# Decoder layer with a mixture of experts on one core: expert loads tied to the landing of a scatter-add, and a gate-up product on unsplit 32-bit operands

## The reference

```python
logits = x @ gate_weight.T                       # 4096 tokens, 128 router columns, 48 kept experts
top_v, top_i = jax.lax.top_k(probs, TOP_K)       # 8 experts of each token, weights normalised
valid = pos < CAP                                # at most 192 tokens of each expert are kept
xb = xb.at[flat_e, pos_c].set(x[tok])[:, :CAP]   # (48, 192, 512)
gu = jnp.einsum('ech,eoh->eco', xb, gate_up_proj)    # (48, 192, 384)
g, u = jnp.split(gu, 2, axis=-1)
h = jax.nn.silu(g) * u
out = jnp.einsum('eci,ehi->ech', h, down_proj)       # (48, 192, 512)
final = jnp.zeros_like(x).at[tok].add(y * w[:, None])
```

## Time and profile before

| | us |
|---|---|
| median of 3 runs (1283.92 to 1286.0) | 1284.0 |
| the profiled execution, its own time | 1285.87 |
| span of the profile | 1284.1 |
| first scatter-add issued | 869.58 |
| VectorE busy, ScalarE busy, TensorE busy over the span | 881.9, 605.8, 1057.7 |

### The profile page before, as it was taken

One profiled execution on the slowest core, in us unless ns is written; L12 is line 12 of the kernel. 1 busy time (PEld: TensorE's weight loads), 2 busy tenths in 40 slices (PEclk: granted clock), 3 DMA queues, 4 the chain that ended last, 5 costly groups with the idle time before them and its releaser, 6 DMA issues.

```text
span 1284.1 us, 24553 instructions
## 1 busy us (share of the span) xinstructions
PE 1057.7 (82%) x6474; PEld 851.7 (66%) x6474; DVE 881.9 (69%) x2462; ACT 605.8 (47%) x1703; POOL 538.5 (42%) x529
## 2 busy tenths in 40 slices
PE   6985898988888988898899897349888888889892
PEld 5773766766766766776677675248777777777682
DVE  5893776777777776777677775437767777777682
ACT  4542344344444443434444444136655666566561
POOL 2123554455455454454445555622332333333233
PEclk9997998899999998889899997669989999999997
DMA  8986335233222112111211211038989999999983
GB/s 304 341 287 243 141 140 179 105 143 139 83 65 80 44 41 75 48 41 41 82 41 41 74 33 39 12 117 252 259 232 256 229 238 253 242 266 247 257 214 49
DMA packets 80110, 191.80 MB, mean 149 GB/s; under 512 B 23175, under 2 KB 23175, under 8 KB 79568
## 3 DMA queue, kind: packets, MB, share of 16 engines
q1 hardware_dynamic: 44112, 130.70, 31.5%
q0 software_dynamic: 31344, 40.07, 14.8%
q10 hardware_dynamic: 4624, 20.68, 4.8%
HBM read 122.30 MB, written 121.87 MB: 190 GB/s over the span
## 4 chain that ended last, share of the span: by engine, by line
issue 37%; POOL 23%; DMA 23%; DVE 8%; PE 3%; POOLq 2%; ACT 1%; another core or an unknown queue 1%; DVEq 0%; SPq 0%; ACTq 0%
DMA layer_out<-qk_both,scatter_idx 20%; POOL slot_records L493 12%; POOL rstd L504 5%; POOL layer_out L539 3%; DVE qk_both L901 3%; DVE diff L896 2%; POOL qk_rot L517 2%; POOL rstd_h L521 1%; DMA slot_records<-row,slot_idx 1%; PE ps L1222 1%; DMA w_raw<-slot_records 1%; PE ps L1083 1%; PE ps L1068 0%; DMA w_raw<-in_weights 0%
## 5 line engine op out<-in xcount | busy, mean ns | idle before, releaser
L493 POOL DMA_INDIRECT slot_records<-row,slot_idx x256 | 257.2, 1005 | 93.1 <-issue 83.8
L539 POOL DMA_INDIRECT layer_out<-qk_both,scatter_idx x96 | 138.1, 1438 | 293.2 <-DVE scatter_idx L1002 224.9
L504 POOL TENSOR_TENSOR rstd<-mv,neg_half 128x1 f32<-128x1 f32 x96 | 79.6, 829 | 256.9 <-DVE mv L842 99.5
L553 ACT ACTIVATE xn_t<-ps 128x512 f32<-128x512 f32 x64 | 38.3, 599 | 177.1 <-PE ps L1068 146.6
L1083 PE MATMUL ps<-w_high,xn_high 128*128 128x512 f32 x384 | 113.4, 417 | 0.7 <-ACT xn_high L553 0.7
L1222 PE MATMUL ps<-w_high 128*128 128x192 f32 x576 | 92.9, 284 | 24.3 <-DVE w_low L988 23.7
L1083 PE MATMUL ps<-w_high,heads_high 128*128 128x512 f32 x128 | 50.1, 527 | 75.3 <-ACT heads_high L553 71.2
L1083 PE MATMUL ps<-w_high,xn_low 128*128 128x512 f32 x384 | 110.1, 409 | 0.0
L1083 PE MATMUL ps<-w_low,xn_high 128*128 128x512 f32 x384 | 108.3, 404 | 0.0
L1222 PEld LDWEIGHTS ps<-w_high 128*128 128x128 f32 x576 | 79.1, 197 | 40.9 <-issue 39.7
L592 ACT ACTIVATE probs<-ps,neg_max_s 128x128 f32<-128x128 f32 x256 | 90.0, 377 | 13.5 <-DVE neg_max_s L798 11.9
(11 more groups left out here) (164 smaller groups left out, 2613.7 us busy)
## 6 DMA issues: line engine op xcount, KB each, us to landing
gu_sb<-in_gate_up SPq DMA_DIRECT2D x48, 768.0 KB
dn_both<-in_down_proj SPq DMA_DIRECT2D x48, 512.0 KB
slot_records<-dn_both ACTq DMA_DIRECT2D x1, 20196.0 KB, 95.9
w_raw<-slot_records SPq DMA_DIRECT2D x48, 420.8 KB
x_ln<-in_x SPq DMA_DIRECT2D x32, 256.0 KB
x_res<-in_x SPq DMA_DIRECT2D x32, 256.0 KB
ctx_t_sb<-in_ctx_t SPq DMA_DIRECT2D x32, 256.0 KB
ctx_sb<-in_ctx_rows SPq DMA_DIRECT2D x32, 256.0 KB
```

Of the source, the lines that this page charges most:

```text
L493: pool.indirect_dma_start(out=records, out_offset=bass.IndirectOffsetOnAxis(ap=slot_idx[:, s.parity, k:k + 1], axis=0), in_=row[:, s.parit ...
L504: pool.tensor_tensor(rstd[:, :], mv[:, 1:2], neg_half[:, 0:1], ALU.pow).then_inc(steps.sem, 1)
L539: pool.indirect_dma_start(out=out, out_offset=bass.IndirectOffsetOnAxis(ap=scatter_idx[:, d.parity, h:h + 1], axis=0), in_=y[:, d.parity, ...
L553: act.activation(dst, src, ACT.Copy).then_inc(steps.sem, 1)
```

## The change

1. Gate-up on unsplit operands. `gu_high`, `gu_low`, `rows_high` and `rows_low` are gone. ScalarE copies the first half of the transposed rows from PSUM to `rows_t` and VectorE the second half; TensorE multiplies `gu_sb` by `rows_t` in 12 matmuls of plain 32-bit numbers.
2. Loads. SP waits until the scatter-add of e - 4 has landed, and then issues in one train the gate-up weights of e, the down weights of e and the rows of e + 1. `gu_sb` is free when the gate-up product of e - 2 is done.
3. GpSimd's waits ahead of the scatter-add stand in another order, the wait for the last scatter-add behind the others.

```diff
             def load_gate_up(e):
                 if e.back(2).exists():
-                    sp.wait_ge(wgu_v.sem, wgu_v.after(e.back(2), "low"))
+                    sp.wait_ge(gup_t.sem, gup_t.after(e.back(2), "second"))
...
-            load_gate_up(Batch(1, 0, E))
-            with sp.Fori(1, E // 2 - 1) as pair:
-                for off in range(2):
-                    load_gate_up(Batch(pair, off + 1, E))
-                    load_rows(Batch(pair, off, E))
-                    load_down(Batch(pair, off, E))
+            load_rows(Batch(1, 0, E))
+            def load_for(e):
+                if e.back(4).exists():
+                    sp.wait_ge(d_add[e.parity], moved(e.back(4), 2))
+                    settled(sp)
+                load_gate_up(e)
+                load_down(e)
+                if e.next().exists():
+                    load_rows(e.next())
+            for off in range(2):
+                load_for(Batch(1, off, E))
+            with sp.Fori(2, E // 2 - 1) as pair:
                 for off in range(2):
-                load_rows(Batch(E // 2 - 1, off, E))
-                load_down(Batch(E // 2 - 1, off, E))
+                    load_for(Batch(pair, off, E))
+                load_for(Batch(E // 2 - 1, off, E))
...
                     if d.back(1).exists():
                         pool.wait_ge(d_add[d.back(1).parity], moved(d.back(1), 2))
-                    pool.wait_ge(dwn_a.sem, dwn_a.after(d, "y0"))
-                    pool.wait_ge(dwn_v.sem, dwn_v.after(d, "y1"))
-                    pool.wait_ge(dwn_i.sem, dwn_i.after(d, "index"))
...
                 if t.exists():
-                    act.wait_ge(d_gu[t.parity], moved(t, 1))
-                    copy(gu_high[:, t.parity, :, :], gu_sb[:, t.parity, :, :], wgu_a)
...
-                    left_by(gu_low[:, t.parity, :, :], gu_sb[:, t.parity, :, :],
-                            gu_high[:, t.parity, :, :]).then_inc(wgu_v.sem, 1)
...
-                        pairs = [(gu_high, rows_high), (gu_high, rows_low), (gu_low, rows_high)]
+                        return product(dst, lambda k: gu_sb[:, u.parity, k, cols], lambda k: rows_t[:, u.parity, k, :])
```

More of the change, by code:

```diff
@@ L59, in back, with next @@
         return Batch(self.pair, self.off - n, self.limit)
+    def next(self):
+        return Batch(self.pair, self.off + 1, self.limit)
 class Steps:
@@ L212, in decoder_layer @@
         weight_of = [sb("weight_even", [HS, 2]), sb("weight_odd", [HS, 2])]
+        rows_t = w_raw[:, :, :, :].rearrange("p a c n -> p (a c n)")[:, 4 * ROW:4 * ROW + 2 * KC * CAP]\
+            .rearrange("p (e c n) -> p e c n", e=2, c=KC)
         def split_buffers(w):
@@ L216, in split_buffers @@
             at = 0
-            for parts, *shape in ((P, 2, KC, 2 * INTER), (P, 2, KC, CAP), (P, 2, 1, DM), (P, 2, 1, DM),
-                                  (P, 2, 1, CAP), (P, 2, 1, CAP)):
+            for parts, *shape in ((P, 2, 1, DM), (P, 2, 1, DM), (P, 2, 1, CAP), (P, 2, 1, CAP)):
                 size = int(np.prod(shape))
@@ L359, in decoder_layer @@
         s_paced = {nc.vector.engine: sem("vector_paced"), nc.gpsimd.engine: sem("pool_paced"),
-                   nc.scalar.engine: sem("scalar_paced")}
+                   nc.scalar.engine: sem("scalar_paced"), nc.sync.engine: sem("sync_paced")}
         def settled(eng):
@@ L530, in expert_turn @@
                 if d.exists():
+                    pool.wait_ge(dwn_i.sem, dwn_i.after(d, "index"))
+                    pool.wait_ge(dwn_a.sem, dwn_a.after(d, "y0"))
+                    pool.wait_ge(dwn_v.sem, dwn_v.after(d, "y1"))
                     if d.back(1).exists():
                         pool.wait_ge(d_add[d.back(1).parity], moved(d.back(1), 2))
-                    pool.wait_ge(dwn_a.sem, dwn_a.after(d, "y0"))
-                    pool.wait_ge(dwn_v.sem, dwn_v.after(d, "y1"))
-                    pool.wait_ge(dwn_i.sem, dwn_i.after(d, "index"))
                     settled(pool)
@@ L670, in expert_turn @@
                 if t.exists():
[L671 to L676, removed]
+                    act.wait_ge(ffn_t.sem, ffn_t.after(t, "rowsT0"))
+                    if t.back(2).exists():
+                        act.wait_ge(gup_t.sem, gup_t.after(t.back(2), "second"))
+                    copy(rows_t[:, t.parity, :, 0:HS], ps[:, 0, 0:KC * HS].rearrange("p (c n) -> p c n", c=KC), ffn_a)
                 if u.exists():
@@ L1013, in expert_turn @@
                 if t.exists():
[L1014 to L1021, removed]
+                    dve.wait_ge(ffn_t.sem, ffn_t.after(t, "rowsT1"))
+                    if t.back(2).exists():
+                        dve.wait_ge(gup_t.sem, gup_t.after(t.back(2), "second"))
+                    dve.tensor_copy(rows_t[:, t.parity, :, HS:CAP],
+                                    ps[:, 1, 0:KC * HS].rearrange("p (c n) -> p c n", c=KC)).then_inc(ffn_v.sem, 1)
                 if u.exists():
@@ L1211, in expert_turn @@
                 if u.exists():
-                    pe.wait_ge(wgu_v.sem, wgu_v.after(u, "low"))
-                    pe.wait_ge(ffn_v.sem, ffn_v.after(u, "low1"))
+                    pe.wait_ge(d_gu[u.parity], moved(u, 1))
+                    pe.wait_ge(ffn_a.sem, ffn_a.after(u, "copied0"))
+                    pe.wait_ge(ffn_v.sem, ffn_v.after(u, "copied1"))
                     if u.back(1).exists():
@@ L1232, in expert_turn @@
                         if t.back(1).exists():
-                            pe.wait_ge(ffn_v.sem, ffn_v.after(t.back(1), f"low{h}"))
+                            if h == 0:
+                                pe.wait_ge(ffn_a.sem, ffn_a.after(t.back(1), "copied0"))
+                            else:
+                                pe.wait_ge(ffn_v.sem, ffn_v.after(t.back(1), "copied1"))
                         for c in range(KC):
```

18 lines of the change are left out of this document (4 added, 14 removed).

## The result

The changed kernel takes 1333.6 us in the median of 4 runs (1332.3 to 1335.7), the kernel before 1284.35 us in 4 runs. The ratio is 1.0383, interval 1.0363 to 1.0402. It is slower, as predicted; the prediction said 1347. The profiled execution's span is 1330.5 us against 1284.1, 46.4 us more.

What follows compares the result with a forecast made beforehand. Bound: a serial DMA chain of 48 scatter-adds, each delayed by loads ahead. Periods of 10.0 us against 8.56, over 44 periods, add 63 us to 1285.9, giving 1349, or 1347 in the median; range 1265 to 1390.

Steps and rivals of the forecast that it cites:

- The first way of adding it up: Expert-stage period: to first data 1.1, loads 5.5, scatter-add 2.6, last packet to landing about 0.6, together 9.8 us.
- the sum: Expert-stage period added from first-data delay, loads, scatter-add and landing, 9.8 us; 10.0 taken, 63 us more over 44 periods.
- the train has no hole in it: SP's loads: 0.67 us from one load to the next, less than any load takes, so no gap.
- a whole period old: Experts' compute waits for loads issued a whole period earlier, so it keeps several us of slack.
- The step that costs each part by itself: Separate costs in the expert stage: gate-up product nothing, GpSimd's waits 0, load train 63 us.
- The engines take turns: DMA engines let scatter-add packets in between loads; period 8.1 us, 1264 us in all; chance 0.15.
- its own sign: Test for DMA engines alternating between queues: a landing 8.5 us or less after the landing before.
- The train runs clean: Serial DMA chain without the loss from small loads at odd times; periods 8.6 to 8.8 us, 1284 to 1295; chance 0.10.
- The slow side: Long periods of 11.2 and 11.8 us become the rule, by TensorE's lower clock or a lagging DMA engine; 1400 to 1427; 0.09.
- Theory A of the experiments: Each follow-up run's own first expectation, not the prediction's; for moved load trains, periods between 7.3 and 8.5 us.

Runs made afterwards that it cites:

- part 2 alone: Kernel before with only the change's load train, split products and GpSimd's waits kept: 1387.4 us, ratio 1.068.
- written pair of e - 3: Changed kernel, load train of e leaving once GpSimd has written both scatter-add DMAs of e - 3, told by a memset: ratio 1.058 to the kernel before.
- the last marked run: Changed kernel, load train of e leaving once GpSimd has written both scatter-add DMAs of e - 4, told by a memset: 1283.7 us, ratio 1.002.

## Why the prediction was right, and where its sizes were off

**The bound and the mechanism.** Both as predicted. The chain of scatter-adds sets the stage: GpSimd starts 0.9 to 1.3 us behind a landing in all 44 periods but one (1.8). The train right behind a landing stands ahead of the next pair. Flights became more even, 6.2 to 8.1 us with a full train ahead, and only q1 packets ran in the five stretches behind 1003. Moving the train to 4.5 us behind a landing takes the whole loss away (1.002 for 1.038), so its place is the cause. That the weights also come some 4 us earlier there can't be it, since in the changed kernel GpSimd never waited for the compute. What the place costs is the 1.6 us a period in which no packet runs.

**The term that was mis-sized** is the period, 10.0 us predicted, 9.78 measured; 44 x 1.22 = 53.8 us instead of 63. The first way of adding it up gave 9.8, and that it came so near is partly luck. From landing to first packet it was 1.2 us (1.1 in the sum), for the loads 5.3 (5.5), for the scatter-add 2.2 (2.6), from last packet to landing 0.3 (0.6). The scatter-add is at the lower bound of the earlier trace rows, where I took the mixed traffic of the earlier trace rows. These four make 9.1 us. The missing 0.7 had no term: the step "the train has no hole in it" left out the engines that idle while the train starts and while the last packets run out. The time in which nothing moves, 1.1 + 0.6 in the sum, was 1.6 us. VectorE's wait ahead of the index copy is 174.0 us in 36 turns, 4.8 us each, as listed.

**What the sum left out.** I let the start of the stage and its first period stand as before. They became 3.3 and 3.4 us shorter, and the measured change is 46 to 49 us, not 54.

**A step that was wrong and changed nothing.** The prediction has the experts' compute wait for loads "a whole period old". The gate-up product doesn't. TensorE's waits from 900 to 1250:

```profile
PE ps L1067 <- DMA gu_sb<-in_gate_up: 68.0, 35, 3.0
```

It waits 1.9 us in each turn for weights that were issued in the same period (issued at 1002.83, product from 1007.29). The slack lies behind it, in the result y, and it is enough in the changed kernel. With the split in between (part 2 alone) or with the train later (written pair of e - 3) it is not, and GpSimd waits for y.

**Part 1** was costed at nothing, and in the changed kernel that is right: halving the product changed no time that can be measured. The product itself takes

```profile
997.84 4.16 PE L1067 MATMUL ps<-w_raw,gu_sb 128*128 128x192 f32 x24 [1.60 <-DMA gu_sb<-in_gate_up]
...
1007.29 5.84 PE L1067 MATMUL ps<-w_raw,gu_sb 128*128 128x192 f32 x24 [2.31 <-DMA gu_sb<-in_gate_up]
```

4.16 us where PEclk is 1.00. In the next turn it takes 5.84 us, out of the predicted 4.0 to 5.0, because PEclk falls to 0.50 from 1008.5 to 1011.5; TensorE had idled 2.3 us before it. The mean from 900 to 1240 is 168.0 / 35 = 4.8 us, for 4.5 taken. What I missed is that part 1 lengthens the life of the buffer. The step that costs each part by itself treated the parts as independent. They are not: 1.339 and 1.068 alone, 1.038 together.

**Part 3** I put between 0 and 7 us gained. Alone it costs 0.9%, and in the changed kernel nothing that can be told (1.036 without it).

**The rivals.** *The engines take turns* fell by its own sign: landings are 8.9 to 10.7 us apart, not 8.5 or less. In the period shown GpSimd's first DMA was written by 1005.00 and its packets began after 1008, when over three quarters of the train had moved. The Trainium skill's rule of turns between queues, a packet at a time ("DMA: Bandwidth & Descriptors", "Queues, rings and completion order"), would let the pair in between the loads. A packet there can hold many of the rows that the profile counts as packets, so how fine the turns are can't be compared. The trace doesn't show turns for the first 1.35 MB of a train. It leaves them open for the last 0.39 MB, which ran beside the scatter-add, and in the last marked run both queues ran side by side for 7 us; the profile doesn't tell whether on one engine. *The train runs clean* was half right: the work got 0.6 us cheaper, and the idle engines cost three times that. *The slow side* had its condition and not its consequence: PEclk is 0.50 to 0.53 for some 3 us in the period shown, yet compute stays hidden.

**Theory A of the experiments** was too hopeful wherever it promised less than 8.5 us. Its periods of 7.5 us and a little more took the scatter-add at the 2.2 us that it has behind the loads, with nothing standing still. No run has both: it is 2.2 to 2.4 us (2.9 behind the written pair of e - 3) with 1.6 us without a packet, or 2.5 to 2.7 with 0 to 0.6. That may also be why the kernel before, uneven as it looks, is hard to beat by moving the train. None of the runs that do the whole work beat it.

## What to carry to other kernels

Before tying a load to an event, ask what else the event releases: here the transfers that started at the same moment as the next link of a serial DMA chain stood in front of it. And look at what the engines do around the event: loads tied to a landing left them empty for 1.6 us each time. When a conversion step is removed, ask when the buffer that it read comes free now, and what stands behind that wait in its queue. A step that is costed at nothing should be costed alone as well as with its partners.

## What was not expected of the hardware

- A load of SP's queue went ahead of GpSimd's scatter-add packets even when it was issued after the scatter-add had started (gate-up load at 1026.23, first DMA at 1025.65; the next 103 packets were the load's). In the run without the wait on the landing, loads got in between the two halves of a pair.
- GpSimd's DMA instruction, 1.41 us as a rule, took 2.9 us in some of the second DMAs of a pair: 11 of 48 in the changed kernel (1005.30, 1025.38 and others), 9 in the last marked run, 1 before. The loads' issue doesn't explain it: in the changed kernel they are issued at the same place ahead of the second DMAs that took 1.41 us, and in the last marked run the one at 1002.02 took 2.89 us with no load issued within 3 us. The cause is open.
- A semaphore increment behind an indirect DMA on GpSimd fired 0.3 us after the first of two DMAs had begun. A memset behind them ended when both were written (memset until 1004.95, second DMA until 1004.91).
- The engine time of 192 rows added to DRAM was 2.2 us where most of the loads were through, 2.6 to 2.7 us beside them, and 2.9 us (280 x 27.2% / 26.3) in the run with the train behind the written pair of e - 3.
- 0.1 us saved at GpSimd's start cost 0.9% in two sets of runs; the cause stays open.
